# Routing three pairs ahead of the shared expert, and the row count inside the loop, in a recurrent layer with 32 routed experts

## The reference

```python
xn = layernorm(x)
# gated recurrence over each sequence, 8 states
combined = xn @ W_in + b_in                 # 256 + 8 columns
embed, state_in = combined[:256], combined[256:]
gate = sigmoid(combined @ W_g + b_g)        # 8
state = gate * state + (1 - gate) * state_in    # a scan over 2048 tokens
s = concat(embed, states) @ W_out + b_out
# experts: 32, four per token, out of the best 4 of 8 groups
scores = softmax(xn @ wg.T); top 4 of the kept groups; w = scores / (sum + 1e-9)
dest = place of the token in its expert, at most cap = 1280 rows
y[token] += w * (silu(xe @ w1) * (xe @ w3)) @ w2
z = silu(xn @ sw1) * (xn @ sw3) @ sw2       # shared expert
out = x + s * silu(y + z)
```

## Time and profile before

| | |
|---|---|
| profiled execution | 1122.59 us, span 1120.7 us |
| PE busy / matmuls | 973.9 us (87%) / 7998 |
| DVE busy | 791.5 us (71%) |
| ACT busy | 581.1 us (52%) |
| POOL busy | 754.3 us (67%) |
| span in 40 slices, PE | `6788878878988489999999999999999999999800` |
| granted clock of PE | `9999999989999699999999999999999999999955` |
| first phase and setup | 0 to about 362 us |
| handover and head of the second phase | about 362 to 401 us |
| second phase at full rate | about 401 to 1060 us |

### The profile page before, as it was taken

How to read it: one execution, slowest core, us unless ns; L and a number is a source line. 1 busy time by engine, 2 the same in 40 slices (tenths; PEclk the granted TensorE clock), 3 DMA queues, 4 the chain that set the end, 5 groups by cost and what they waited for, 6 DMA issues and landing times.

```text
span 1120.7 us, 29269 instructions
## 1 busy us (share of the span) xinstructions
PE 973.9 (87%) x7998; PEld 946.7 (84%) x7998; DVE 791.5 (71%) x2547; ACT 581.1 (52%) x1109; POOL 754.3 (67%) x602
## 2 busy tenths in 40 slices
PE   6788878878988489999999999999999999999800
PEld 4677777777887489999999999999999999999800
DVE  5767777767777457777776776777777777777558
ACT  4768768768886234444444444444444444444233
POOL 1167777777777755666767756766757667676785
PEclk9999999989999699999999999999999999999955
DMA  9133433333334777878877788788887878887579
GB/s 311 62 123 136 145 132 140 141 133 137 141 133 146 229 165 179 167 148 159 167 169 153 142 177 167 139 182 169 159 185 143 181 165 178 168 176 146 69 243 372
DMA packets 157683, 184.18 MB, mean 164 GB/s; under 512 B 19337, under 2 KB 147378, under 8 KB 157618
## 3 DMA queue, kind: packets, MB, share of 16 engines
q0 software_dynamic: 56000, 79.89, 37.4%
q1 hardware_dynamic: 100992, 103.50, 30.1%
q10 hardware_dynamic: 626, 0.01, 0.0%
HBM read 85.63 MB, written 101.35 MB: 167 GB/s over the span
## 4 chain that ended last, share of the span: by engine, by line
PE 72%; DVE 10%; ACT 7%; issue 6%; DMA 2%; POOL 2%; SPq 0%; DVEq 0%; ACTq 0%; POOLq 0%
PE h L713 13%; PE h L715 13%; PE h L714 13%; PE yb L733 7%; PE yb L731 7%; PE yb L732 7%; PE xt L697 6%; DVE s_all L1526 2%; DVE s_all L1523 2%; ACT rows L929 1%; POOL slot_rows L589 1%; DVE act L1227 1%; DVE raw L1236 1%; PE gb L791 1%; PE ls L770 1%
## 5 line engine op out<-in xcount | busy, mean ns | idle before, releaser
L606 POOL DMA_INDIRECT y_sum<-y_more,y_idx x220 | 351.3, 1597 | 197.9 <-DMA y_sum<-yw,y_idx 76.7
L713 PE MATMUL h<-xh,w_hl 128*128 (+1 forms) x1392 | 411.4, 296 | 5.8 <-DVE w_hl L1214 3.7
L715 PE MATMUL h<-xl,w_hl 128*128 (+1 forms) x1392 | 396.1, 285 | 0.0
L714 PE MATMUL h<-xh,w_hl 128*128 (+1 forms) x1392 | 394.5, 283 | 0.0
L589 POOL DMA_INDIRECT slot_rows<-rows,dest_idx x256 | 258.5, 1010 | 116.6 <-issue 73.7
L1000 ACT ACTIVATE acth<-act 128x512 fp32r<-128x512 f32 x174 | 109.7, 630 | 314.9 <-PE yb L733 303.2
L713 PEld LDWEIGHTS h<-xh,w_hl 128*128 128x128 f32 x1392 | 266.0, 191 | 7.9 <-issue 6.8
L714 PEld LDWEIGHTS h<-xh,w_hl 128*128 128x128 f32 x1392 | 266.3, 191 | 0.0
L715 PEld LDWEIGHTS h<-xl,w_hl 128*128 128x128 f32 x1392 | 266.1, 191 | 0.0
L1231 DVE TENSOR_TENSOR actl<-act,acth 128x512 fp32r<-128x512 f32 x174 | 120.7, 694 | 181.0 <-ACT acth L1000 180.8
L731 PE MATMUL yb<-w_hl,acth 128*128 128x256 f32 x696 | 197.2, 283 | 6.2 <-DVE actl L1231 3.5
(11 more groups left out here) (223 smaller groups left out, 1407.3 us busy)
## 6 DMA issues: line engine op xcount, KB each, us to landing
rows<-slot_rows SPq DMA_DIRECT2D x143, 289.0 KB, 3.6
raw<-L_ffn_w SPq DMA_DIRECT2D x96, 256.0 KB, 3.1
slot_rows<-rows SPq DMA_DIRECT2D x32, 289.0 KB, 3.5
x_all<-L_attn_x SPq DMA_DIRECT2D x16, 512.0 KB, 6.0
y_sum<-yw SPq DMA_DIRECT2D x32, 256.0 KB
out<-s_all SPq DMA_DIRECT2D x32, 256.0 KB, 6.5
slot_rows<-rows,dest_idx POOLq DMA_INDIRECT x256
y_sum<-y_more,y_idx POOLq DMA_INDIRECT x220
```

What stands on the lines that cost most here:

```text
L606: pool.indirect_dma_start(y_dram, bass.IndirectOffsetOnAxis(y_idx[:, buf, t:t + 1], 0), y_out[buf][:, t, :], None, bounds_check=token_boun ...
L713: mm(out, high, xh[:, k, cols], start=(k == 0), stop=False)
L714: mm(out, low, xh[:, k, cols], start=False, stop=False)
L715: ins = mm(out, high, xl[:, k, cols], start=False, stop=(k == KD - 1))
```

## The change

The loop keeps its 32 iterations of the shared expert, but everything else in iteration p is now done for pair `p + LEAD`, LEAD = 3, and the routing is that of the next group. Pairs 0, 1 and 2 and the routing of group 0 are done in setup. The states go into four buffers; x has four places too (two in `xh`, `xl`, two in `w_hl[0]`, which is free in this phase). Setup is re-ordered: the first x load is cut in two, the gates' weights are folded first, GpSimd does some fills, two tiles are normalised by VectorE, the shared weights are loaded into `rows`. The count is issued in iteration 30, behind `down(29)` on TensorE and behind `act_low(30)` on VectorE. ScalarE splits the first expert's weights in iteration 31, ahead of `silu(31)`. TensorE does `down(31)` behind the transposes of the first expert's rows. SyncE stores z of pairs 30 and 31 among the first loads of rows.

```diff
+LEAD = 3
 # SyncE
-            with sp.Fori(0, A_PAIRS) as q:
+            with sp.Fori(0, A_PAIRS - 2) as q:
+                store_z(q)
...
             sp.wait_ge(counts_ready, 2)
-            sp.wait_ge(zero_ready, 1)
-            store_zeros(0)
+            sp.wait_ge(fills_ready, FILLS)
+            store_zeros(0, zero_first.unsqueeze(1).to_broadcast([P, 2, ROW]))
+            store_z(A_PAIRS - 2)
             sp.wait_ge(scattered[0], ALL_SCATTERED)
             load_rows(0, 0, 3, False, zeros_too=True, by_group=True, values=first_values)
             load_rows(0, 1, 0, False, by_group=True)
+            store_z(A_PAIRS - 1)
             sp.wait_ge(scattered[1], ALL_SCATTERED)
             load_rows(0, 2, 1, False, by_group=True)
 # TensorE
             for p in range(A_PAIRS):
-                if has_next:
-                    transpose_tokens(p + 1)
+                ahead = p + LEAD
+                if ahead < A_PAIRS:
+                    transpose_tokens(ahead)
...
-                add_states(p, i)
+                add_states(p)
                 def meanwhile():
-                    if has_next:
-                        gate_inputs(p + 1)
+                    if ahead < A_PAIRS:
+                        gate_inputs(ahead)
                     if p > 0:
                         down(p - 1, w_hl[1], [(z_ready, 2 * p - 2)])
-                    if has_next:
-                        logit_transposes(p + 1)
-                    if i == 1:
-                        positions(g)
+                    if ahead < A_PAIRS:
+                        logit_transposes(ahead)
+                    if p % 2 == 1 and p // 2 + 1 < GROUPS:
+                        positions(p // 2 + 1)
+                    if p == A_PAIRS - 2:
+                        count_rows()
...
-            down(A_PAIRS - 1, w_hl[1], [(z_ready, 2 * A_PAIRS - 2)])
-            pe.wait_ge(seen_ready, GROUPS + 1)
-            mm(cnt, ones[:, :], seen[:, :], start=True, stop=True)
...
             look_ahead(0, PAIRS - 1, 1)
+            down(A_PAIRS - 1, w_hl[1], [(z_ready, 2 * A_PAIRS - 2)])
             pe.wait_ge(z_ready, 2 * A_PAIRS)
 # ScalarE, loop
                 take_s(p)
+                if p == A_PAIRS - 1:
+                    sc.wait_ge(h3_ready, A_PAIRS - 2)
+                    sc.wait_ge(ls_ready, 2 * (A_PAIRS - 2))
+                    split_high(w_hl[0], 32)
                 silu(p)
...
-            split_high(w_hl[0], 32)
 # VectorE, loop (the other steps keep their places, with p + LEAD and the next group)
-                    if g in (0, 1):
-                        statistics(4 + 2 * g)
+                    if g == 1:
+                        statistics(4)
+                        statistics(5)
...
+                if p == A_PAIRS - 2:
+                    count_rows()
+                    split_low(w_hl[0], 4, range(2))
```

More of the change, by code:

```diff
@@ L1034, in _ @@
             take_logits(0)
-            normalise(0, range(2, 4))
-            states_high(0, 0)
+            take_logits_t(1)
+            take_logits(1)
+            sc.wait_ge(fills_ready, FILLS)
+            exps(0)
+            normalise(1, range(2))
+            states_high(0)
+            gates(1)
+            sc.wait_ge(setup_pe, 4)
+            done(av(wch[:, :, :], ls[0][:, :].rearrange("p (k c) -> p k c", k=KD), ACT.Copy))
+            sc.wait_ge(setup_loaded, 32)
+            done(av(wo[0:SD, :], s_wout8, ACT.Copy))
@@ new lines, in _ @@
+            done(av(wo[32:32 + SD, :], s_wout8, ACT.Copy))
+            sc.wait_ge(setup_pe, 5)
+            done(av(wo[96:97, :], bias_row, ACT.Copy))
+            assert n_setup[0] == SETUP_ACT
+            xhigh(2, x_high(2))
+            normalise(1, range(2, 4))
+            split_shared()
+            take_logits_t(2)
+            states_high(1)
+            gates(2)
+            take_logits(2)
+            sc.wait_ge(bias_low_ready, 1)
+            sc.dma_start(wo[97:98, :].bitcast(F32), bias_low).then_inc(bias_moved, 16)
@@ L1215, in split_low, with split_low_shared, xlow @@
                                     ALU.subtract).then_inc(wl_ready, 1)
-            def xlow(p, cols, wait=None):
+            def split_low_shared():
+                for n in range(3):
+                    ve.wait_ge(wh_ready, n + 1)
+                    v.tensor_tensor(w_hl[1][:, 2 * n + 1, :, :], shared_raw(n), w_hl[1][:, 2 * n, :, :].bitcast(F32),
+                                    ALU.subtract).then_inc(wl_ready, 1)
+            def xlow(p, high, low, wait=None):
                 ve.wait_ge(xh_ready, p + 1)
@@ L1356, in _ @@
+            ve.wait_ge(setup_act, GATES_ACT)
+            done(v.tensor_tensor(wgl[:, :, 0:SD], folded.rearrange("p (k c) -> p k c", k=KD),
+                                 wgh[:, :, 0:SD].bitcast(F32), ALU.subtract))
+            assert n_setup[0] == GATES_DVE
+            xlow(1, x_high(1), x_low(1))
             norm_prepare(1)
             norm_finish(1)
-            recurrence(0, 0, True)
+            route_centre(0)
+            recurrence(0)
+            route_groups(0, 0)
+            route_experts(0)
```

533 lines of the change are left out of this document (316 added, 217 removed).

## The result

The changed kernel takes 1128.74 us (median of 20 runs), the kernel before 1124.86 (20 runs beside them). The ratio is 1.0044, 95% interval 1.0030 to 1.0058: slower by 4 to 5 us, where 2.4 us less was forecast. The profiled execution took 1128.02 us, span 1126.2, that is 5.5 us above the span before.

A forecast was written before the change was run, and what follows sets the result against it. VectorE, the engine with the fewest waits, was taken to bound the first phase. Loop lead -10.5, handover +9.3 and head pairs -1.2 summed to -2.4 us: 1120.8 us, 8-in-10 range 1111 to 1128.5 (the forecast's own 1115 to 1126).

The forecast's parts named there:

- Setup: Setup into the loop: centre of group 0 at 19.9 us, of group 1 at 46.3, against 35.56 and 60.07 before.
- Group 1's iterations hold four statistics calls in place of two: 22.07 + 3.2.: Loop, centre of group 1 to 2: two more statistics calls add 3.2 us to 22.07; centre of group 2 at 71.6.
- From there both kernels do the same per group.: Loop from the centre of group 2 on: 0 us change per group, so the loop stays 10.5 us ahead.
- The 3.0 us stay.: Loop iterations: VectorE's wait for the logits stays 3.0 us in each group, since the order of steps is untouched.
- Handover: From loop to experts: count, row loads, `down(31)` and store of z in a chain make `up(32)` 9.3 us later.
- Head pairs: The three pairs behind `up(32)`, 20.75 us before: a wait for rows goes, gain 1.2 us, bounds 0 and 2.5.
- Rival C (slower): Setup: slower hops between engines and a late bias DMA start the loop 7.5 us later: 1128.3 or more; chance 0.13.
- A: Rival, loop: iterations get shorter, 7.0 us over 13 groups, 7.5 over 14, giving 1113 us; chance 0.23.
- B: Rival, handover: it hides, `up(32)` comes 17.8 us earlier than forecast, giving 1103 us; chance 0.08.
- D: Rival, experts' first rows: a load waits for GpSimd's scatters, so the gain goes, giving 1123 us; chance 0.07.
- the 10.5 us: Loop: the lead over the kernel before, forecast from the centre of group 2 on.

The follow-up runs named there:

- Experiments 1 to 4: Changed kernel with gap filled by 48 matmuls, 1.0005; statistics calls spread, 1.0007; all four in setup, 1.0019. Kernel before with calls doubled, 1.0012. Ratios to kernel before.
- Experiments 5, 9 and 10: Handover edits to the changed kernel: both together in 5 and 10; singly on slower chips in 9, `down(31)` earlier 0.9961, VectorE's z wait later 0.9938 of kernel before.
- experiment 5: Changed kernel with `down(31)` ahead of the first rows' transposes and VectorE's wait for z behind the first xl: 0.9993 of the kernel before.
- experiment 10: Changed kernel, on slower chips, with `down(31)` ahead of the first rows' transposes and VectorE's z wait behind the first xl: 0.9945 of the kernel before.

## Why the prediction was wrong

- *Setup.* Right: 20.30 (19.9) and 45.88 (46.3), through hops with TensorE's matmuls 0.21 us apart. The second is in part luck: the bias row was there 0.9 earlier than I had it (`add_states(0)` at 38.98, not 39.9), and the last link was VectorE's xl, done at 42.85, in place of TensorE's half of `up`, for which I had 43.1. A table load was followed by the next step at once there too (16.38 + 1.28, then 17.68).
- *"Group 1's iterations hold four statistics calls in place of two: 22.07 + 3.2."* This step failed. The interval took 29.96 us in place of 25.3. The calls cost 3.8 (3.2 forecast), and TensorE's idle time behind them, which the sum had at nothing, another 4.1, by its clock. Experiments 1 to 4 move, take away or fill it and get the time back or lose it.
- *"From there both kernels do the same per group."* Failed by 2.6 us (269.5 against 266.9 from group 2 to 15). VectorE's list is the same, TensorE's gaps aren't; low time and time go together over eight traces, but no run isolates this part, and its cause stays open. At the end, where no statistics are due, a group takes 18.80 (18.86 before), as forecast.
- *"The 3.0 us stay."* Right nearly everywhere: 2.97, but for 4.32, 4.22 and 3.85 in three groups, the ones with a lower clock.
- *Handover.* Right in its chain and nearly in size (+10.2 for +9.3). The count started 5.8 us behind the low part of pair 29 (5 to 7 expected); TensorE was empty for 15.5 us (8.46 and 7.01), broken by `down(31)`. Experiments 5, 9 and 10 show both links.
- *Head pairs.* -1.8 for -1.2.
- *Rival C (slower).* Its bound held (the time was past 1128.3), its mechanism did not: group 1's centre came at 45.88, far from 54. The slow TensorE that it looked for in setup sat one group later.
- *A, B, D.* A did not happen. B's 17.8 us were not there, and D's waits for GpSimd neither.

The handover alone made a gain impossible unless nearly all of the 10.5 us was kept; I gave the forecast a range of 1115 to 1126 on a term that I had costed on one engine only.

## What to carry to other kernels

Work added to the engine that others wait for can cost twice, as the two doubled calls did here: its own time (3.8 us), and what the idle engine behind it loses by its clock (4.1). So spread such work out over iterations, or give TensorE something to do (which helped on one kind of chip, 1.0005, and not on the other, 1.0027), and read the granted clock of each stretch, not only the waits. And when the last step of one phase gates the first of the next, look for what is merely in order ahead of it: here two steps put in another place were worth about 5 us (5.7 by the ratios of experiment 5, 4.7 in experiment 10).

## What was not expected of the hardware

- TensorE's clock fell behind idle stretches of 1.9 to 2.3 us too, in some groups and not in others, and in other groups in the trace of experiment 5, which has the same lists there (17.1 us of low time against 34.2). For one, a gap of 2.19 us at 78.69 had no fall behind it in the changed kernel, and one of 2.30 at 78.29 in experiment 5 had (low from 81.1 to 84.5).
- The same kernel takes 1124 us on some chips and 1238 to 1246 on others, all of it in the first phase. Engines stand there at times with nothing that releases them, TensorE up to 1.8 us between single matmuls; these rows are a small part of the 100 us. A change can be worth something else there: 1.0044 (1.0030 to 1.0058) on the one, 0.9978 (0.9948 to 1.0007) on the other.
